# A two-layer mixture-of-experts kernel: the wait for the scatter one tile back is taken out of the second layer's dispatch

## The reference, cut to what matters

```python
x = x + _L0_ffn_ref(_L0_cond_ref(fside_BxS_0, cond_1024, x, coeffs), ...)
x = x + _L1_ffn_ref(_L1_cond_ref(x, cond_1024, Wx, Wh, b), ...)

def _L0_ffn_ref(x, ...):                  # 32 x 128 tokens of 128 features
    probs = softmax((x @ Wg + bg) / 5.0); vals, idx = top_k(probs, 2)     # 2 of 8 experts
    y = sum over the chosen experts of gate * (gelu(x @ W1[e] + b1[e]) @ W2[e] + b2[e])

def _L1_cond_ref(x, h0, Wx, Wh, b):       # a recurrence over the 128 steps of a sequence
    h = tanh(x[:, t] @ Wx + b + h @ Wh)   # step after step, 32 sequences side by side

def _L1_ffn_ref(x, ...):
    logits = layer_norm(x) @ gate_w.T; tk_probs, tk_idx = top_k(softmax(logits), 2)
    out = swiglu(x, sWg, sWu, sWd)        # shared expert, for every token
    out = out + w[:, e:e+1] * swiglu(x, Wg[e], Wu[e], Wd[e])              # for e in range(8)
```

## Time and profile before

| what | us |
|---|---|
| median of 3 runs | 570.84 |
| the 3 runs | 564.85, 570.84, 573.53 |
| the profiled execution, its own time | 567.24 |
| its span, first to last instruction | 565.4 |

### The profile page before, as it was taken

How to read it: one execution, slowest core, us unless ns; L and a number is a source line. 1 busy time by engine, 2 the same in 40 slices (tenths; PEclk the granted TensorE clock), 3 DMA queues, 4 the chain that set the end, 5 groups by cost and what they waited for, 6 DMA issues and landing times.

```text
span 565.4 us, 10030 instructions
## 1 busy us (share of the span) xinstructions
PE 433.3 (77%) x2406; PEld 336.5 (60%) x2406; DVE 335.4 (59%) x1315; ACT 202.4 (36%) x652; POOL 278.3 (49%) x289
## 2 busy tenths in 40 slices
PE   5887744481878888885799999998894799998910
PEld 3545523470766666664568877775673688877710
DVE  4878534643555555554348777788575366665635
ACT  1121012300555544443155555554342245454400
POOL 2255772474255555555001666654645555555530
PEclk9758565666799999998799999999799799999975
DMA  6980110012332222211332111111422233222149
GB/s 169 330 258 28 52 49 24 29 52 65 92 104 77 80 81 81 77 44 37 121 117 75 39 39 39 44 35 39 118 60 65 80 92 86 81 76 59 44 147 326
DMA packets 48270, 49.64 MB, mean 88 GB/s; under 512 B 8748, under 2 KB 37367, under 8 KB 48087
## 3 DMA queue, kind: packets, MB, share of 16 engines
q1 hardware_dynamic: 38422, 30.02, 19.2%
q0 software_dynamic: 8640, 17.84, 9.5%
q10 hardware_dynamic: 1152, 1.14, 0.6%
HBM read 27.85 MB, written 21.12 MB: 87 GB/s over the span
## 4 chain that ended last, share of the span: by engine, by line
PE 64%; DVE 10%; issue 9%; another core or an unknown queue 5%; DMA 4%; ACT 3%; POOL 2%; SPq 2%; ACTq 1%; DVEq 0%; POOLq 0%
PE banks L1199 54%; PE banks L1203 7%; PE banks L1287 3%; DMA parts<-results 2%; POOL parts L469 1%; POOL results L513 1%; SPq L393 1%; DMA results<-stream,y_dest 1%; DMA xpow<-in_fside_BxS 1%; ACT act_row L592 1%; ACT act_col L598 1%; DVE state_lo L1067 1%; SPq L403 1%; DVE stream L980 1%
## 5 line engine op out<-in xcount | busy, mean ns | idle before, releaser
L513 POOL DMA_INDIRECT results<-stream,y_dest x142 | 136.4, 960 | 124.3 <-DVE stream L983 94.8
L482 POOL DMA_INDIRECT regions<-parts,pos x64 | 63.6, 994 | 53.3 <-DVE pos L902 26.5
L482 POOL DMA_INDIRECT regions<-first_w,pos x64 | 62.1, 970 | 44.7 <-ACT hT L615 27.2
L598 ACT COPY act_col<-banks 128x256 f32<-128x256 f32 x146 | 54.5, 374 | 53.0 <-remote 40.7
L1203 PE MATMUL banks<-const_sb,act_row 128*128 128x128 f32 x292 | 57.3, 279 | 8.1 <-ACT act_col L598 6.8
L1203 PEld LDWEIGHTS banks<-const_sb,act_row 128*128 128x128 f32 x292 | 40.8, 144 | 30.0 <-issue 14.1
L615 ACT ACTIVATE hT<-banks,pcol 128x32 f32<-128x32 f32 x128 | 36.9, 288 | 54.3 <-PE banks L1199 44.2
L674 ACT ACTIVATE silu_row<-banks 128x256 f32<-128x256 f32 x75 | 29.1, 388 | 74.4 <-PE banks L1199 45.9
L1199 PE MATMUL banks<-first_w,act_col 128*128 x284 | 46.0, 286 | 10.4 <-DVE stream L983 7.1
L1199 PEld LDWEIGHTS banks<-hT,wh 128*128 128x128 f32 x256 | 39.2, 188 | 24.1 <-ACT hT L615 17.0
L1199 PE MATMUL banks<-first_w,state 128*128 x142 | 48.1, 422 | 6.9 <-issue 4.4
(11 more groups left out here) (187 smaller groups left out, 856.5 us busy)
## 6 DMA issues: line engine op xcount, KB each, us to landing
parts<-results SPq DMA_DIRECT2D x16, 512.0 KB, 4.0
hT<-regions SPq DMA_DIRECT2D x71, 65.0 KB
wgu<-regions SPq DMA_DIRECT2D x71, 65.0 KB
results<-stream,y_dest POOLq DMA_INDIRECT x142
base<-in_x SPq DMA_DIRECT2D x12, 128.0 KB, 3.3
regions<-const_sb SPq DMA_DIRECT2D x18, 65.0 KB
first_w<-in_L_ffn_W SPq DMA_DIRECT2D x1, 1024.0 KB, 6.6
first_w<-in_L_ffn_W SPq DMA_DIRECT2D x2, 512.0 KB, 8.5
```

The costliest lines, as they stand in the source:

```text
L482: pool.indirect_dma_start(regions[layer], bass.IndirectOffsetOnAxis(ap=poss[layer][q][:, t, k:k + 1], axis=0), hrows[layer][:, q, t, k, :] ...
L513: pool.indirect_dma_start(results[layer], bass.IndirectOffsetOnAxis(ap=y_dest[:, s:s + 1], axis=0), y_row[:, s, :], None).then_inc(results ...
L598: nc.scalar.copy(act_col[:, j % ACT_RING, :], act_turned_ps[:, j % 2, 0:HID]).then_inc(act_copied[layer], 1)
```

## The change

The three lines that compute `sent` and wait for it in layer 1 are taken out of `send`; the indirect DMA and its increment stay. All other waits on `scattered` stay as they are.

```diff
                 ring = 2 + layer
                 q = n % ring
-                sent = tiles_on(layer, q, n) + t
-                if layer and t:
-                    pool.wait_ge(scattered[layer][q][k], 16 * sent)
                 pool.indirect_dma_start(regions[layer], bass.IndirectOffsetOnAxis(ap=poss[layer][q][:, t, k:k + 1], axis=0),
                                         hrows[layer][:, q, t, k, :], None).then_inc(scattered[layer][q][k], 16)
```

## The result

The changed kernel takes **584.42 us** (median of 4 runs, 583.84 to 585.87) against 567.85 us for the kernel before in the same measurement (4 runs, 564.75 to 573.53). The ratio is 1.034, with a 95% interval of 1.030 to 1.039. The forecast was 569, so it was wrong, and the time lies above its range.

What follows compares the result with a forecast made beforehand. The recurrence, with TensorE busy throughout, was taken to pace everything and GpSimd to follow. All terms summed to 0 on a 565.4 us span, a 567.2 execution; 569 was taken between that and the median 570.84, range 563 to 575.

Steps and rivals of the forecast that it cites:

- no 1.83 among them: Sign in the recurrence's stream: scatter starts, alternating 1.26 and 1.83 us apart before, should all be 1.26 apart.
- block 6's eight: Sign: block 6's eight scatters should take 8.9 us from first to last start rather than 10.5.
- The median dispatch: Sign: the median duration of a scatter's dispatch on GpSimd should stay at 0.96 us.
- rival C: Scatter dispatches in the stream stretch and GpSimd falls behind: slower, 574.5 us; chance 0.07.
- the rule of the Trainium skill: GpSimd cannot write descriptors while VectorE holds their shared port pair, so closer scatters would meet longer dispatches; hardly any expected.
- Rival D: Steps or the queue space the scatters, so the 1.26 and 1.83 alternation stays and the time is 569 us; chance 0.05.
- SyncE still waits for the table: Ahead of the slots' loads SyncE waits for VectorE's table, so scatters landing 1.65 us earlier gain 0.
- A: SyncE's first load waits for the landing, not the table, and starts up to 1.65 us sooner: about 567.4 us; chance 0.07.
- Added: more scatters in flight: Term for 3 or 4 scatters in flight in layer 1 instead of at most 2: 0, at most 0.44 us each.
- Rival B: ScalarE's stalls in the slots, 14.0 us between 427 and 452, go with the waits: 555 us, 2.7% faster; chance 0.06.
- a stall or two of 2.5 us is met or missed, in either direction: Smaller effect beside the stalls in the slots: later work shifts by a microsecond, so ScalarE's stalls may change either way.

Runs made afterwards that it cites:

- e5: The changed kernel itself, run on a chip without pauses against the kernel before: 482.35 against 481.77 us, ratio 1.001.
- e17: Kernel before, landing wait kept, plus a 128x400 memset ahead of each result but the first: 556.72 against 568.03 us, ratio 0.985.
- e12: Changed kernel with the landing wait kept for blocks 0 to 5 only, chip with pauses: 576.46 us, ratio 1.013 to the kernel before.
- e13: Changed kernel with the landing wait kept for blocks 6 and 7 only, chip with pauses: 590.25 us, ratio 1.023 to the kernel before.
- e14: Changed kernel with a 128x400 memset ahead of each scatter that had the wait, chip with pauses: 564.2 us, ratio 0.996 to the kernel before.
- e16: The changed kernel again, on the same chip with pauses as e14 and e15: 580.82 us, ratio 1.028 to the kernel before.
- e10: Changed kernel with a 128x288 memset ahead of each scatter that had the wait, chip with pauses: 584.28 us, ratio 1.029 to the kernel before.
- e8: Kernel before with 140 small DMAs on SyncE's queue in the recurrence, chip with pauses: 623.85 us, ratio 1.086 to the kernel before.
- e15: Kernel before with each result also waiting for the landing of the result two back, chip with pauses: 575.99 us, ratio 1.019.

## Why the prediction was wrong

**What held.** The reading of who waits for whom held. Without the wait, scatters follow at 1.26 to 1.27 with no 1.83 among them, and block 6's eight take 8.93 us from first to last start (forecast 8.9). Line 479 of the changed kernel (ns min/median/max, first and last start), which answers to the earlier trace rows:

```profile
L479 POOL DMA_INDIRECT regions<-parts,pos x64: 956/962/1404, 29.2 to 134.1; - x64
L479 POOL DMA_INDIRECT regions<-first_w,pos x64: 956/962/1036, 309.6 to 462.7; - x64
```

The median dispatch stayed at 0.962, so rival C (stretched dispatches) is out; and the rule of the Trainium skill that the prediction weighed ("SBUF — State Buffer", section "SBUF: two separate sides") shows nothing here: the longest scatter of layer 1 is 1,036 ns in both traces, though they follow more closely. Rival D (the pace doesn't change) is out as well. SyncE still waits for the table and not for a landing, which answers to the earlier trace rows:

```profile
SPq L378 <- DVE table L955: 103.5, 1, 103.5
```

and it passes the landings at 404.15 in 0.03 us, so A, a slack handed on, did not happen. On a chip without pauses the forecast of no change held: 1.001 for the change (e5), and 0.9998 and 1.0001 for its halves.

**What failed.** Two steps, with one cause.

*"Added: more scatters in flight", taken at 0.* I bounded this term by the duration of the dispatch on GpSimd alone (0 to 0.44 us each), as if a closer dispatch could cost only its own engine. What it cost was time in which ScalarE waits for late increments of TensorE: 9.6 us in the recurrence, and a part of the 4.3 after it; the two stretches are 14 of the 16.6 us. Layer 0 was the right place to look, and I read the wrong row of it. 51 of its 63 intervals between scatters are 1.26 or 1.27 us, at a median dispatch of 962 ns, but the stage takes 104.5 us (29.3 to 133.8) where e5, on a chip without pauses, takes 88.9 (28.9 to 117.8). I had asked what the dispatches cost GpSimd there, not what the other engines were doing meanwhile.

*Rival B and the argument against it.* B came nearest: it connected ScalarE's unexplained stalls with the scatters. I had its sign wrong, and I dismissed the connection because layer 0's slots have 13 such gaps "where no scatter of tokens is issued". True, but results are indirect DMAs of GpSimd too, at 1.27 us from start to start, four in a row ahead of each pause. Those 13 gaps were the best evidence for the mechanism, and e17, which spaces the results at 1.58 and has none, shows it. With it in hand a sum could have been made, an estimate in hindsight: runs of five scatters at 1.27 in the stream's blocks, one pause of about 2 us of path each, is 5 to 6 blocks x 2 = 10 to 12 us, and one more for block 6: slower by 2 to 3%.

The sentence "a stall or two of 2.5 us is met or missed, in either direction" came nearest to the case, and stalls met more often shared 4 in 100 with C's long dispatches.

**What is shown and what is not.** Shown: the loss goes with the two places of the waits (e12, e13); in the recurrence it is ScalarE waiting for increments of TensorE that are recorded up to 2.13 us after the product's end, while those of the other engines are on time; and it goes when the dispatches are spaced at 1.58 us without any landing wait (e14 against e16). The same spacing removes the same pauses at another line (e17). Open: what carries the hold-up from GpSimd's dispatches to TensorE's increments, why it sets in after four or five at 1.27, why 1.49 still has it, and why some chips don't have it at all. Over half of the records of DMAs' increments, 16 to a DMA, are missing in traces of chips with pauses (3,870 before and 3,999 after, against 8,179 in e5). That goes with the pauses; which of the two brings the other, or whether one thing brings both, no run tells.

## What to carry to other kernels

A wait that nobody waits behind may still be setting a pace on which other engines depend: before costing its removal at nothing, look for gaps of other engines whose releaser the profile cannot name, and for what all of them have just ahead of them in time, by kind of instruction and not by line. Where the releaser is "remote", compare the time of the increment with the end of the instruction that makes it: that tells a slow consumer from a late signal. Where GpSimd issues four or more indirect DMAs at 1.27 us and ScalarE or VectorE waits 2 to 3 us for a product that has ended, space them (1.58 us here) and measure. Do it on more than one chip: the same edit was worth nothing on one kind and 3% on the other.

## What the runs showed of the hardware

- On some chips, where the kernel before takes 566 to 575 us instead of 482, increments of TensorE's semaphores are held and then come in a burst, 0.03 to 0.06 us apart, while those of VectorE, ScalarE and GpSimd come within 0.04 us of the instruction's end. ScalarE or VectorE waits 2 to 5 us for them.
- It goes with runs of four or more indirect DMAs of GpSimd at 1.27 us. At 1.49 the recurrence's pauses come later in a block and are shorter (e10), at 1.58 there is none (e14).
- An idle pause can speed a kernel up: 128x400 memsets, with which GpSimd is busy for 99 of 111 us, shorten the first layer's slots from 118.9 to 110.6 us.
- Small DMAs of another queue can lengthen a wait for a landing: with 140 of them on SyncE's, the first scatters that wait come 4 to 9 us apart instead of 1.3 to 1.8, and the kernel takes 8.6% longer (e8).
- TensorE's granted clock fell to 0.50 (1.2 GHz) within a stretch of unbroken work and made the step 1.28 instead of 0.79 (e15, e17).
